# The second layer's queries, keys and values from 16-bit parts in three products, with the order of all steps laid out anew

## What is computed

```python
xn = _layernorm(x)
x = x + attention0(xn) + ffn0(xn)     # 32 heads of 8, causal, rotary; gelu gating through 8-bit floats
xn = _layernorm(x)
x = x + attention1(xn) + ffn1(xn)     # ternary weights, rms norm
```

```python
q = (x @ wq.T).reshape(b, s, H, HD)   # HIDDEN 256, H 16, HD 16
k = (x @ wk.T).reshape(b, s, H, HD)
v = (x @ wv.T).reshape(b, s, H, HD)
q, k = apply_rope(q, inv_freq), apply_rope(k, inv_freq)
scores = einsum('bshd,bstd->bsht', q, k) / sqrt(HD)   # softmax over t, then the values
```

## Time and profile before

| | us |
|---|---|
| median of 3 runs | 604.13 (604.02 to 604.8) |
| the profiled execution | 603.83 |
| its span, first to last instruction | 602.1 |
| TensorE busy | 560.9 |
| ScalarE busy | 467.7 |
| VectorE busy | 444.4 |
| GpSimd busy | 257.8 |

### The profile page before, as it was taken

How to read it: one execution, slowest core, us unless ns; L and a number is a source line. 1 busy time by engine, 2 the same in 40 slices (tenths; PEclk the granted TensorE clock), 3 DMA queues, 4 the chain that set the end, 5 groups by cost and what they waited for, 6 DMA issues and landing times.

```text
span 602.1 us, 13153 instructions
## 1 busy us (share of the span) xinstructions
PE 560.9 (93%) x5035; PEld 290.9 (48%) x5085; DVE 444.4 (74%) x905; ACT 467.7 (78%) x605; POOL 257.8 (43%) x318
## 2 busy tenths in 40 slices
PE   4687898999999999999989999999999999999997
PEld 2332433444455455554535555555444454356665
DVE  6899998879787764785987868648454646467967
ACT  2499899987779988899668787887889797874451
POOL 4773966145626335233765638225052240261200
PEclk9699999999999999999999999999999999999999
DMA  8630110030430233001104032340410501334542
GB/s 285 248 106 2 36 36 1 1 53 3 70 53 11 47 44 53 1 2 29 19 0 73 0 54 49 51 53 10 80 20 2 88 1 29 51 54 80 106 62 56
DMA packets 150912, 30.38 MB, mean 50 GB/s; under 512 B 133952, under 2 KB 149568, under 8 KB 150848
## 3 DMA queue, kind: packets, MB, share of 16 engines
q1 hardware_dynamic: 150272, 29.19, 24.5%
q10 hardware_dynamic: 576, 0.33, 0.3%
HBM read 19.02 MB, written 10.49 MB: 49 GB/s over the span
## 4 chain that ended last, share of the span: by engine, by line
PE 65%; DVE 16%; ACT 8%; issue 6%; DMA 3%; POOL 1%; SPq 1%; DVEq 0%; ACTq 0%
PE psV L693 16%; PE psS L679 7%; ACT Pt L934 4%; PE psA L842 3%; PE psS L796 3%; PE psA L861 2%; PE psB L842 2%; PE psC L842 2%; DVE ga L1296 1%; DMA stage<-in_wg 1%; PE psA L758 1%; PE psC L861 1%; PE psB L861 1%; PE psC L730 1%; DVE ga L1293 1%
## 5 line engine op out<-in xcount | busy, mean ns | idle before, releaser
L934 ACT ACTIVATE Pt<-psS 128x1024 f32<-128x1024 f32 x288 | 280.1, 1031 | 54.1 <-PE psS L679 29.6
L693 PE MATMUL psV<-Pt,vaug 128*32 128x512 f32 x1152 | 146.5, 602 | 3.7 <-DVE ob L1256 1.5
L1591 POOL TENSOR_SCALAR_AFFINE_SELECT Pt<-Pt 128x1024 f32<-128x1024 f32 x64 | 74.7, 1191 | 52.9 <-ACT Pt L934 52.6
L679 PE MATMUL psS<-qTf,kTf 32*128 32x512 f16 x576 | 72.5, 387 | 3.1 <-ACT Pt L934 1.5
L679 PEld LDWEIGHTS psS<-qTf,kTf 32*128 32x128 f16 x576 | 19.2, 91 | 75.5 <-ACT Pt L934 37.7
L693 PEld LDWEIGHTS psV<-Pt,vaug 128*32 128x32 f32 x1152 | 26.1, 108 | 50.1 <-issue 36.1
L1646 POOL TENSOR_TENSOR ss<-ss,mhalf 128x1 f32<-128x1 f32 x16 | 9.0, 564 | 92.0 <-DVE ss L1425 91.9
L983 ACT ACTIVATE stage<-psS 128x1024 f32<-128x1024 f32 x32 | 31.0, 1022 | 7.9 <-PE psS L796 7.5
L1637 POOL TENSOR_TENSOR r<-qk,cos 128x256 f32<-128x256 f32 x16 | 14.2, 888 | 47.4 <-ACT qk L967 47.4
L1582 POOL TENSOR_TENSOR QXf<-rt,QXf 128x512 f16<-128x512 f32 x16 | 19.5, 1216 | 26.1 <-ACT QXf L921 26.1
L1620 POOL TENSOR_SCALAR rs<-mv 128x1 f32<-128x1 f32 x16 | 4.5, 283 | 52.4 <-DVE mv L1319 52.3
(11 more groups left out here) (375 smaller groups left out, 1290.9 us busy)
## 6 DMA issues: line engine op xcount, KB each, us to landing
qkvscr<-rqkv SPq DMA_DIRECT2D x16, 384.0 KB, 2.6
G<-qkvscr SPq DMA_DIRECT2D x24, 128.0 KB, 3.8
stage<-in_wg SPq DMA_DIRECT2D x4, 512.0 KB, 7.8
oscr<-o SPq DMA_DIRECT2D x16, 128.0 KB, 3.0
w8g<-qkvscr SPq DMA_DIRECT2D x16, 128.0 KB, 3.7
at<-oscr SPq DMA_DIRECT2D x16, 128.0 KB, 2.2
out<-yout SPq DMA_DIRECT2D x16, 128.0 KB, 2.7
x<-in_x SPq DMA_DIRECT2D x1, 1536.0 KB, 12.0
```

Of the source, the lines that this page charges most:

```text
L679: e.matmul(psS[j], kd[32 * j:32 * j + k, h, 128 * at:128 * at + 128], qd[32 * j:32 * j + k, 4 * h:4 * h + 4, :].rearrange("p s n -> p (s n ...
L693: ins = e.matmul(psV[32 * j:32 * j + 32, :], vaug[:, at, j, 32 * h:32 * h + 32], Pt[(4 * Q + j) % NP], start=(kb == 0 and h == 0), stop=(k ...
L934: e.activation(flat(Pt4[:, u % NP:u % NP + 2, :]), flat(psS4[:, j:j + 2, :]), ACT.Exp, scale=scale).then_inc(S["exp"], 1)
L1591: e.affine_select(out=p, in_=p, pattern=[[0, 8], [1, 128]], compare_op=ALU.is_ge, fill=0.0, base=0, channel_multiplier=-1).then_inc(S["mas ...
```

## The change

The second layer's queries, keys and values come from 16-bit parts. The weights, times 64 (`WUP`), are split once: `wh` (ScalarE) casts them, `wl` (VectorE) writes the difference; both parts lie where the 32-bit weights lay, and the raw weights are loaded into `stmp`, so the first `tg` waits for `wl`. `xn1Tc` now writes the high and the low part of the input itself, both from the bank, and `xl` is gone from GpSimd. `qkv1` is six products of 16 bits (high by high, high by low, low by high, over two halves) in place of two of 32. `qk1c` and `v1c` divide by 64. A new test joins the others: `wsq` squares the weights' high parts, `wsum.0` and `wsum.1` add them over blocks of 64 rows on TensorE, `wmin` takes the least, and `rng` compares it with `SMALLEST`. The second pass keeps the 32-bit products and loads the weights again.

```diff
@@ -27,6 +27,8 @@
 NP = 8
 LOW, HIGH, LARGE = 1e-36, 1e30, 3e38
 UP = 64.0
+WUP = 64.0
+SMALLEST = WUP * WUP * 2.0 ** -9
 WIDEST = 600.0
 MAGIC = 12582912.0
 TWO_PI = 2.0 * np.pi
...
-    "pool": "rs0 rope ql QUADS ge4:0 ge4:1 xf rs1 xl ro1p rsg",
+    "pool": "rs0 rope ql QUADS ge4:0 ge4:1 xf rs1 ro1p rsg",
...
-    "wo0": lambda n: ("xa", n + 1), "up": lambda m: ("fh" if m % 2 else "g", m // 2 + 1), "down": lambda n: ("yff", n + 1), "flagT": lambda n: ("flag", 1),
+    "wo0": lambda n: ("xa", n + 1), "up": lambda m: ("fh" if m % 2 else "g", m // 2 + 1), "down": lambda n: ("yff", n + 1), "flagT": lambda n: ("flag", 1), "wsum": lambda m: ("wmin", m + 1),
...
-ln1 xn1 xn1Tc v1c ro1 ro2 gTq m1 gTm o1r o1 sg hh ssm hx hTc at1Tc yo yout osum flag rng rngb
-zero gz zf rs0 rope ql mask ge4 xf rs1 xl ro1p rsg w8a""".split()
+wh wsq wsum ln1 xn1 xn1Tc xn1f wl wmin v1c ro1 ro2 gTq m1 gTm o1r o1 sg hh ssm hx hTc at1Tc yo yout osum flag rng rngb
+zero gz zf rs0 rope ql mask ge4 xf rs1 ro1p rsg w8a""".split()
...
+
+        wparts = flat(wqkv1[:]).bitcast(F16).rearrange("p (q a n) -> p q a n", q=2, a=2)
...
+        wraw = flat(stmp[:])[:, 0:1536].rearrange("p (a n) -> p a n", a=2)
+        wsquares = flat(stmp[:])[:, 0:768].bitcast(BF16).rearrange("p (a n) -> p a n", a=2)
...
@@ -476,7 +481,7 @@
             def load_rest():
                 xt = A["x"].rearrange("(t p) c -> p t c", p=128)
                 e.dma_start(x[:, 4:NT, :], xt[:, 4:NT, :]).then_inc(S["d_x2"], 16)
-                e.dma_start(wqkv1[:], A["wqkv1"].rearrange("(a p) n -> p a n", p=128)).then_inc(S["d_w1"], 16)
+                e.dma_start(wraw, A["wqkv1"].rearrange("(a p) n -> p a n", p=128)).then_inc(S["d_w1"], 16)
                 e.dma_start(wo1_w[:], A["wo1"].rearrange("(a p) n -> p a n", p=128)).then_inc(S["d_w1"], 16)
 
             def wg(k):
...
+                e.dma_start(wqkv1[:], A["wqkv1"].rearrange("(a p) n -> p a n", p=128)).then_inc(S["d_w1"], 16)
...
@@ -748,15 +754,34 @@
                 w.wait_ge("xn1", n + 1)
                 transpose_pair(shared("xn1T", n), xn1_b[n % len(xn1_b)], "xn1T")
 
+            def wsum(m):
+                c0, c1 = ((0, 512), (512, 768))[m]
+                w.wait_ge("zero", 5)
+                w.wait_ge("wsq", 1)
+                bank = shared("wsum", m)
+                e.matmul(bank[:, 0:c1 - c0], blockb[:], wsquares[:, 0, c0:c1], start=True, stop=False)
+                e.matmul(bank[:, 0:c1 - c0], blockb[:], wsquares[:, 1, c0:c1], start=False, stop=True).then_inc(S["wsum"], 1)
+
             def qkv1(m):
                 n, part = divmod(m, 2)
                 c0, c1 = ((0, 512), (512, 768))[part]
-                src = xn1T_b[n % len(xn1T_b)]
-                w.wait_ge("xn1Tc", 2 * n + 1)
-                w.wait_ge("d_w1", 32)
-                bank = shared("qkv1", m)
-                e.matmul(bank[:, 0:c1 - c0], src[:, 0, :], wqkv1[:, 0, c0:c1], start=True, stop=False)
-                e.matmul(bank[:, 0:c1 - c0], src[:, 1, :], wqkv1[:, 1, c0:c1], start=False, stop=True).then_inc(S["qkv1"], 1)
+                if n < NT:
+                    src = xhs[n % len(xhs)]
+                    w.wait_ge("xn1Tc", 2 * n + 2)
+                    w.wait_ge("wh", 1)
+                    w.wait_ge("wl", 1)
+                    bank = shared("qkv1", m)
+                    for k, (pt, q, a) in enumerate(((0, 0, 0), (0, 1, 0), (0, 0, 1), (0, 1, 1), (1, 0, 0), (1, 0, 1))):
+                        ins = e.matmul(bank[:, 0:c1 - c0], src[:, pt, 128 * a:128 * a + 128], wparts[:, q, a, c0:c1],
+                                       start=(k == 0), stop=(k == 5))
+                    ins.then_inc(S["qkv1"], 1)
+                else:
+                    src = xn1T_b[n % len(xn1T_b)]
+                    w.wait_ge("xn1f", n - NT + 1)
+                    w.wait_ge("d_w1", 48)
+                    bank = shared("qkv1", m)
+                    e.matmul(bank[:, 0:c1 - c0], src[:, 0, :], wqkv1[:, 0, c0:c1], start=True, stop=False)
+                    e.matmul(bank[:, 0:c1 - c0], src[:, 1, :], wqkv1[:, 1, c0:c1], start=False, stop=True).then_inc(S["qkv1"], 1)
 
             def transpose_groups(bank, n, s, sem):
                 for j in range(4):
...
-                w.wait_ge("xl", n + 1)
...
                 w.wait_ge("ro1", 2 * (n + 1 - len(qk1)))
                 bank = psM[filled["qkv1", 2 * n] % len(psM)]
-                e.activation(qk1[n % len(qk1)][:], bank[:], ACT.Copy).then_inc(S["qk1c"], 1)
+                e.activation(qk1[n % len(qk1)][:], bank[:], ACT.Copy, scale=1.0 / WUP if n < NT else 1.0).then_inc(S["qk1c"], 1)
+
+            def wh(n):
+                w.wait_ge("d_w1", 32)
+                e.activation(wparts[:, 0, :, :].rearrange("p a n -> p (a n)"), flat(wraw), ACT.Copy, scale=WUP).then_inc(S["wh"], 1)
+
+            def wsq(n):
+                w.wait_ge("wl", 1)
+                e.activation(wsquares.rearrange("p a n -> p (a n)"), wparts[:, 0, :, :].rearrange("p a n -> p (a n)"),
+                             ACT.Square).then_inc(S["wsq"], 1)
 
             def gTk(n):
...
+                w.wait_ge("wl", 1)
...
@@ -1328,18 +1362,35 @@
 
             def xn1Tc(n):
                 bank = psM[filled["xn1T", n] % len(psM)]
+                dst = xhs[n % len(xhs)]
                 w.wait_ge("xn1T", n + 1)
-                w.wait_ge("qkv1", 2 * (n + 1 - len(xn1T_b)))
-                w.wait_ge("xl", n + 1 - len(xn1T_b))
-                e.tensor_copy(flat(xn1T_b[n % len(xn1T_b)][:]), bank[:, 0:256]).then_inc(S["xn1Tc"], 1)
+                w.wait_ge("qkv1", min(2 * (n + 1 - len(xhs)), 2 * NT))
                 w.wait_ge("gu", 4 * (n + 1 - len(xhs)))
-                e.tensor_copy(xhs[n % len(xhs)][:, 0, :], bank[:, 0:256]).then_inc(S["xn1Tc"], 1)
+                e.tensor_copy(dst[:, 0, :], bank[:, 0:256]).then_inc(S["xn1Tc"], 1)
+                w.wait_ge("xn1Tc", 2 * n + 1)
+                e.tensor_tensor(dst[:, 1, :], bank[:, 0:256], dst[:, 0, :], ALU.subtract).then_inc(S["xn1Tc"], 1)
+                if n >= NT:
+                    w.wait_ge("qkv1", 2 * (n + 1 - len(xn1T_b)))
+                    e.tensor_copy(flat(xn1T_b[n % len(xn1T_b)][:]), bank[:, 0:256]).then_inc(S["xn1f"], 1)
+
+            def wl(n):
+                w.wait_ge("d_w1", 32)
+                w.wait_ge("wh", 1)
+                e.scalar_tensor_tensor(wparts[:, 1, :, :].rearrange("p a n -> p (a n)"), flat(wraw), WUP,
+                                       wparts[:, 0, :, :].rearrange("p a n -> p (a n)"), ALU.mult, ALU.subtract).then_inc(S["wl"], 1)
+
+            def wmin(m):
+                bank = psM[filled["wsum", m] % len(psM)]
+                c = (512, 256)[m]
+                w.wait_ge("wsum", m + 1)
+                e.tensor_reduce(hl[:, 19 + m:20 + m], bank[:, 0:c], AX.X, ALU.min).then_inc(S["wmin"], 1)
 
             def v1c(n):
                 bank = psM[filled["qkv1", 2 * n + 1] % len(psM)]
                 w.wait_ge("qkv1", 2 * n + 2)
                 w.wait_ge(f"d_vw{n % 2}", 16 * (n // 2))
-                e.tensor_copy(rqkv[n % 2][:, 2, :], bank[:, 0:256]).then_inc(S["v1c"], 1)
+                e.tensor_scalar(rqkv[n % 2][:, 2, :], bank[:, 0:256], 1.0 / WUP if n < NT else 1.0, None,
+                                ALU.mult).then_inc(S["v1c"], 1)
 
             def half1(k, s):
...
+                w.wait_ge("wsum", 2)
...
-                e.tensor_reduce(hl[:, 15:16], widest[:], AX.X, ALU.max).then_inc(S["rng"], 1)
+                e.tensor_reduce(hl[:, 17:18], widest[:], AX.X, ALU.max).then_inc(S["rng"], 1)
-                e.tensor_scalar(hl[:, 12:13], hl[:, 15:16], WIDEST, None, ALU.is_lt).then_inc(S["rng"], 1)
+                e.tensor_scalar(hl[:, 12:13], hl[:, 17:18], WIDEST, None, ALU.is_lt).then_inc(S["rng"], 1)
+                w.wait_ge("wmin", 2)
+                e.tensor_scalar(hl[:, 14:16], hl[:, 19:21], SMALLEST, None, ALU.is_gt).then_inc(S["rng"], 1)
...
+                e.tensor_reduce(hl[:, 16:17], hl[:, 6:16], AX.X, ALU.min).then_inc(S["rngb"], 1)
...
@@ -1621,11 +1675,6 @@
                 w.wait_ge("rs1", 2 * n + 1)
                 e.tensor_tensor(rs[:, 1:2], rs[:, 0:1], mhalf[:], ALU.pow).then_inc(S["rs1"], 1)
 
-            def xl(n):
-                dst = xhs[n % len(xhs)]
-                w.wait_ge("xn1Tc", 2 * n + 2)
-                e.tensor_tensor(dst[:, 1, :], flat(xn1T_b[n % len(xn1T_b)][:]), dst[:, 0, :], ALU.subtract).then_inc(S["xl"], 1)
-
             def ro1p(n):
```

All five lists are written anew (789 to 791 steps on TensorE, 419 to 421 on ScalarE, 689 to 692 on VectorE, 162 to 146 on GpSimd, 88 on SP). The places of the new steps, and the tail of two lists:

```diff
 act
+tc.0 qh.0 tde.0 exp.0 qh.1 tde.1 g.0 exp.1 sq.0 wh.0 fh.0 tc.1 th.0 g.1 sq.1 exp.2
+exp.18 tg.0 g.7 wsq.0 exp.19 fh.7
 dve
+qkvc.5 yff.1 ln0.6 ge3.4 wl.0 tw.4 q0.4 ob.2 tw.5
+v1c.0 att.3 tcs.5 xn1.1 wmin.0 qTc.5 ge3.7 tw.10 xn1Tc.1 ge1.8 xnTc.7 tw.11 hh.0 ro1.0 sg.1 hh.1 ro2.0 wmin.1
 pe
+qxT.11 wsum.0 td.10 qk.24 pv.23 tr.10 td.11 xn1T.1 qk.25 pv.24 xnT.7 tr.11 gu.1 qk.26 gu.2 gu.3 wsum.1
-qk.143 gu.52 dn1.10 hxT.22 hxT.23 S1.11 xn1T.14 pv.142 pv.143 PV1.11 gT.24 gT.25 o1T.11 gu.53 obT.15
```

(3 more changed lines are left out.)

21 lines of the change are left out of this document (10 added, 11 removed), and 261 rows, old and new, of the table ORDER.

## The result

| | us | against the kernel before |
|---|---|---|
| changed kernel, median of 5 runs | 602.09 (601.21 to 602.4) | 0.9954, interval 0.994 to 0.9969 |
| kernel before beside it, 5 runs | 604.8 | |
| changed kernel again, on another chip (e17) | 601.45 | 0.9958, interval 0.9944 to 0.9972 |
| profiled execution, its span | 602.12, 600.4 | |

The change makes the kernel 2.7 us faster. The forecast was 5 us; the measured 602.1 us lies inside the stated range, but the gain is about half of the one forecast. In what follows a ratio is turned into microseconds with 604.4 for the kernel before.

The account below looks back on a forecast made before the run. It took TensorE as nearly the limit from 105 to 550 us, between an opening held by VectorE and ScalarE and a dependent tail. 603.83 - 7.5 - 1.35 + 0.86 + 3.05 = 598.9, given as 599.0; range 592.5 to 605.5.

Parts of the forecast that it names:

- The products: Second layer's query, key and value matmuls on TensorE: shorter 16-bit groups save 7.5 us on the chain.
- at the heads: Start of the product groups: 0.09 us less at each of 15 groups on the chain, 1.35 us saved.
- The opening: Before some 110 us: weights' parts charged half of 6.1, 3.05 us, plus 0.86 for the sum of squares on TensorE.
- The order at 0: All five rewritten lists: new order valued at 0, with one transfer of 4.3 us on either side.
- The first rival: Slower: opening paid in full, ScalarE's exponentials replace the array in the middle, half of 8.8 left; 606.4 us, chance 0.17.
- The second: No change: opening paid in full, order loses two or three microseconds at a tail transfer; 603.9 us, chance 0.10.
- The fourth, the port lock: Without GpSimd's xl steps, VectorE's two-input instructions are no longer held: up to 2.2 us more, 590.9 with the third; chance 0.05.
- the tests named: Trace signs: TensorE busy about 9 us less, six 16-bit instructions a group, idle near 11 us from 105 to 550.
- The signs of being wrong: More waits before L679 or L693, the tail's at<-oscr transfer past 7 us, or TensorE waiting for xhs.

Follow-up runs that it names:

- e17: The changed kernel again, without an edit, on another chip: 601.45 us, ratio 0.9958.
- e9: Kernel before, old order, with the new products; the weights' parts are a constant brought by the weights' transfer, no test of sums: 599.7 us, ratio 0.9926.
- e5: Kernel before, its order and 32-bit products, with the opening's new work added into spare memory and unused: 609.6 us, ratio 1.0088.
- e1: All of the change (new products and new work, no xl steps) in the order of the kernel before: 604.65 us, ratio 1.0007.
- e2: Kernel before with the changed kernel's order alone, new steps left out and xl kept: 608.85 us, ratio 1.0074.
- e10: Changed kernel without the opening's new work; the weights' parts are a constant brought by the weights' transfer: 602.43 us, ratio 0.9962.
- e18: Changed kernel with one swap on SP's queue and two VectorE opening steps put back where the kernel before had them: 604.69 us, ratio 1.0007.
- e8: Changed kernel with only the first four of the six products of each group: 598.71 us, ratio 0.9907.
- e7: Changed kernel without the opening's new work; the weights' parts are a constant written by a GpSimd memset: 604.5 us, ratio 0.9998.
- e6: Kernel before, old order, with the new products, without the opening's new work; a GpSimd memset writes the weights' parts: 601.77 us, ratio 0.9958.
- e11: Changed kernel with 62 ScalarE steps narrowed from 512 to 128 columns: 598.56 us, ratio 0.9906.

## Why the forecast was too low

**The products** (failed: the overlap, and with it the size). The prices were right, and the sum was 7.5 us on the chain and 1.35 at the heads, 8.85 together. The step that failed is "on the chain it is 11 x 0.427 + 13 x 0.213 = 7.5 us": a piece on the chain was credited in full, as if nothing stood right behind it. Measured in the old order it is 4.5 (e9) to 4.9 us (e5 to e1), although the array's busy time falls by 9.4; in the new order it is 6.8 (e2 to e10). Other waits stood there; ScalarE's exponentials are the ones that the runs price, and VectorE's load and the lists take a part. The two readings that misled are "98% of the middle" and the 65% of the chain: neither says how soon another engine is reached. The test named for this, that TensorE's idle time from 105 to 550 us stays near 11, is met by the letter (445 - 434.96 = 10.0), but the 11 was too high by the records that are missing; between ob.3 and ob.15 of e5 and e1 it grows by 3.3.

**The opening** (failed, both ways). I charged 3.05 + 0.86 = 3.9 for the new work. In the old order it costs 5.3, against an upper bound of 6.1 + 0.86 = 7.0; in the new order, nothing. The half was a mean between two cases, each of which comes near in one order.

**The order at 0** (failed). With the new work in, the order is worth 3.1 us in the change's favour; alone it costs 4.5. The 0 hid losses in the opening and the middle and a gain in the tail. The forecast saw the gain: it names about 3 us of work that no longer stand in the tail, and a transfer that no longer waits, and then values both at nothing. The tail got shorter by 3.7 to 4.2 us. It did not see the loss: counting places in array work shows nothing of it, because in the first 110 us the other engines' lists decide too, as e18's 4.9 us for two moves on VectorE's list show.

The two errors offset each other in part, and how much of the shortfall falls to each depends on the way taken from one kernel to the other. By the old order: products -4.5, work +4.9, order -3.1. By the new one: order +4.5, products -6.8, work -0.4. Either way the sum is -2.7, and either way the products fall short of 8.85. That 602.1 lies in the stated range is no merit of the sum.

**The rivals.** The first rival, opening in full and the products at half, describes e1 by its parts: half of 8.85 is 4.4, and 4.5 was measured; the work costs 5.3 of the 7.0 that it was charged. So it had e1 at 2.6 us over the kernel before, where 0.4 was measured. It was rightly described and wrongly placed, since it is the change without its order. The second had a loss in the tail; the transfer at<-oscr is not on any wait that the changed trace shows near at1T.12. The fourth, the port lock, was to let VectorE gain from the xl steps that went. The runs show no such gain. In one order, e5 with the xl steps has 23.8 us of VectorE's hx step and e1 without them 23.9; with the three other large two-input steps it is 93.5 and 94.9 us. The fall of the hx step from 23.8 (L1431) to 21.5 in the changed kernel (L1482) comes mostly with the order: e2, which keeps the xl steps, has 22.4.

**By the tests named.** Six 16-bit instructions a group at the forecast price: right. A fall of TensorE's busy time by about 9 us: right, 9.4 and 9.0 behind ob.3 in the pairs with complete traces. TensorE's work by 105 us, 80.7 before, 39.13 + 39.72 = 78.85 after: a fall of 1.9, between the 0 and 3 that were named. The signs of being wrong: in the changed kernel the score products wait 1.7 us for ScalarE against 1.5 before, the attention's second products less than before, no wait of TensorE is for xhs, and no at<-oscr of the tail takes longer than 2.6 us to land. None of them showed, and the forecast was wrong all the same: the waits that ate the gain grow between e5 and e1, not between the kernel before and the change.

## What to carry to other kernels

A chain piece has two prices: what it takes, and how far it can shrink before another engine ends the wait. Here the array was some 98% busy in the middle and the next engine 84%, and of the array work removed about a half was kept as time in the old order, three quarters in the new one, and 2.9 of 7.1 us at the next cut (e8). So full credit is an upper bound; probe it by removing more in a kernel that may compute less (e8 cost one line). Where a kernel's order is written out, new work has no price of its own: the same 6 us cost 5.3 in one order and nothing in another, so look for the holes before charging it, and judge an order only together with the work that it was laid out for, stretch by stretch: a zero can be a loss and a gain. And compare the counts of instructions before the busy times of two traces are subtracted.

## What was new of the hardware

A GpSimd memset, which reads nothing, can hold a VectorE instruction for as long as it lasts: a 0.43 us cast took 2.56 us beside one of 2.65 us (e7), a 0.20 us step 2.01 (e6), and two kernels lost some 2 us each to that one memset (e6 to e9, e7 to e10). The Trainium skill has it so ("SBUF — State Buffer", section "SBUF: two separate sides") for a VectorE instruction that uses two ports for its one input: the port pair that the two engines share goes to whichever starts first, for its whole instruction, and the other is blocked. For a VectorE instruction with two SBUF inputs the Trainium skill limits the lock to a GpSimd instruction that reads SBUF. The trace agrees with both: both instructions held have one input, the cast ends 0.29 us after the memset and the step of e6 0.05 us after, and the two-input step beside the memset of e7 took 0.90 us against 0.91 without. That the cast ran on two ports, no trace shows. So an idle stretch of GpSimd is not free room.

The Trainium skill also warns that the busy share of the products is no good measure of how near a kernel is to its limit ("Perfetto Trace Analysis", section "Identifying the Most-Contended Engine"), and tells one to work on the most-contended engine first. The runs agree in so far as neither share foretold the gain: TensorE, busy 93% of the span, gave 2.9 us for 10.2 us of work at the forecast's prices (e8), ScalarE, at 78%, 2.9 us for 18 (e11). Per microsecond taken away the busier engine gave more, but under a third of it. The Trainium skill's reason for the warning, that pipelined products look smaller in the trace, is not what these two runs test.
